# A fused state-space, attention and feed-forward kernel: the opening of attention on VectorE with the residual's seeds in eight transfers, and a last stage that takes its output products by alternating quarters

## What is computed

```python
def block_one(x):                       # stage A: a selective scan (Mamba)
    xz = x @ in_proj_w.T ; conv ; silu ; softplus steps ; scan over 512 positions, 16 states
    return y * silu(z) @ out_proj_w.T

def _gate(x, Wsel):                     # sigmoid scores, the best 2 of 8 experts kept
    s = jax.nn.sigmoid(jnp.einsum('bsd,hed->bhse', x, Wsel))
    _, idx = jax.lax.top_k(s, K)
    return s * jax.nn.one_hot(idx, E).sum(-2)

def _moe_attn(x, Wq, Wk, Wv, Wo, Wsel_v, Wsel_o):     # stage B
    q, k = _rope(x @ Wq), _rope(x @ Wk)               # 16 heads of 64
    v = jnp.einsum('bsd,bhse,hedp->bhsp', x, _gate(x, Wsel_v), Wv)
    att = softmax(q k^T / sqrt(64))
    return jnp.einsum('bhsp,bhse,hepd->bsd', att @ v, _gate(x, Wsel_o), Wo)

src = _ln(src + _moe_attn(src, ...), ln1_g, ln1_b)    # stage C
src = _ln(src + relu(src @ W1 + b1) @ W2 + b2, ln2_g, ln2_b)

x = x + _layernorm(block_one(_layernorm(x)))
x = x + _layernorm(block_two(_layernorm(x)))
```

## Time and profile before

| | |
|---|---|
| median of 3 runs | 3919.82 us (3918.64 to 3920.61) |
| the profiled execution's own time | 3914.3 us |
| its span | 3912.5 us |
| PE busy | 3596.8 us (92%) |
| PEld busy | 2472.4 us (63%) |
| DVE busy | 3211.4 us (82%) |
| ACT busy | 2037.4 us (52%) |
| POOL busy | 2722.2 us (70%) |
| mean granted TensorE clock | 0.980 |

### The profile page before, as it was taken

The page is one execution under the profiler, slowest core; times in us unless marked ns, Lnnn a source line. Parts: engine busy times, 40 slices in busy tenths (PEclk is TensorE's granted clock), DMA queues, the critical chain, the costliest instruction groups (busy, mean ns, idle before and its releaser), DMA issues. The chain is left out here.

```text
span 3912.5 us, 55524 instructions
## 1 busy us (share of the span) xinstructions
PE 3596.8 (92%) x15792; PEld 2472.4 (63%) x15792; DVE 3211.4 (82%) x3580; ACT 2037.4 (52%) x3795; POOL 2722.2 (70%) x2852
## 2 busy tenths in 40 slices
PE   6999999998669999999999999999999999999797
PEld 3444444444247777777777777777777777777586
DVE  6999989998748888888888887888887888888697
ACT  5666666666334454445454545444444445444455
POOL 4877788787657676677777677767677767776344
PEclk9999999999979999999999999999999999999898
DMA  2110111011043242323232323233323332222111
GB/s 78 54 49 27 65 70 71 20 56 60 25 159 81 56 110 55 81 60 105 55 87 78 77 64 100 60 76 89 76 60 77 88 73 68 66 70 68 43 33 49
DMA packets 76054, 267.78 MB, mean 68 GB/s; under 512 B 9326, under 2 KB 38894, under 8 KB 53072
## 3 DMA queue, kind: packets, MB, share of 16 engines
q1 hardware_dynamic: 74944, 262.83, 24.8%
q0 software_dynamic: 1040, 4.19, 0.3%
HBM read 247.85 MB, written 19.14 MB: 68 GB/s over the span
## 5 line engine op out<-in xcount | busy, mean ns | idle before, releaser
L384 POOL TENSOR_TENSOR state<-state,c_rows 128x1024 f32<-128x1024 f32 x256 | 604.6, 2365 | 215.1 <-DVE state L848 212.7
L848 DVE TENSOR_TENSOR_SCAN state<-dA,ps_a 128x1024 f32<-128x1024 f32 x256 | 585.2, 2286 | 46.8 <-PE ps_a L524 21.8
L1104 POOL TENSOR_TENSOR qk_full<-vg 128x512 f32<-128x512 f32 x256 | 330.1, 1289 | 254.3 <-DVE vg L1489 254.1
L715 ACT ACTIVATE dA<-dt,a_neg 128x511 f32<-128x511 f32 x512 | 338.8, 714 | 311.4 <-DVE state L848 309.5
L1489 DVE TENSOR_TENSOR vg<-ps_b,gates 128x1024 f32<-128x1024 f32 x256 | 313.6, 1225 | 221.2 <-PE ps_b L1215 188.6
L524 PE MATMUL ps_a<-state,ident 128*128 128x512 f32 x1024 | 481.9, 593 | 0.4 <-POOL state L384 0.4
L1213 PE MATMUL ps_b<-ogT_high,wo_high 128*128 128x512 f32 x1024 | 415.6, 406 | 33.8 <-POOL ogT_low L1117 27.2
L1378 ACT ACTIVATE prob<-ps_b,negmax 128x512 f32<-128x512 f32 x512 | 343.6, 676 | 188.9 <-DVE negmax L1495 188.9
L1213 PE MATMUL ps_b<-wv_high,xT_high 128*128 128x512 f32 x1024 | 414.3, 405 | 3.8 <-POOL wv_low L1097 3.8
L1215 PE MATMUL ps_b<-ogT_high,wo_low 128*128 128x512 f32 x1024 | 408.2, 399 | 0.0
L1214 PE MATMUL ps_b<-ogT_low,wo_high 128*128 128x512 f32 x1024 | 405.9, 396 | 0.0
(11 more groups left out here) (245 smaller groups left out, 8449.9 us busy)
## 6 DMA issues: line engine op xcount, KB each, us to landing
ogT_low<-gates_scratch SPq DMA_DIRECT2D x128, 512.0 KB, 6.3
wide_high<-gates_scratch SPq DMA_DIRECT2D x128, 512.0 KB, 9.7
xT<-xT_scratch SPq DMA_DIRECT2D x65, 512.0 KB, 3.3
c_rows<-c_scratch SPq DMA_DIRECT2D x32, 1024.0 KB, 5.4
wv<-in_wv SPq DMA_DIRECT2D x8, 1024.0 KB, 11.5
wo<-in_wo SPq DMA_DIRECT2D x8, 1024.0 KB, 13.5
x_in<-in_x SPq DMA_DIRECT2D x8, 512.0 KB, 5.1
x_a<-in_x SPq DMA_DIRECT2D x8, 512.0 KB, 7.1
```

Of the source, the lines that this page charges most:

```text
L384: pool.tensor_tensor(state, state, c_rows[:, n, :].unsqueeze(1).to_broadcast([P, HALF, S]), ALU.mult).then_inc(hc_done, 1)
L715: act.activation(dA[s % RING][:, m, 1:S], dt[par][:, HALF * f + m, 1:S], ACT.Exp, scale=a_neg[:, HALF * f + m, n:n + 1]).then_inc(dA_done, 1)
L848: dve.tensor_tensor_scan(h[s % RING][:, :, :].rearrange("p c s -> p (c s)"), dA[s % RING][:, :, :].rearrange("p c s -> p (c s)"), ps[:, DB ...
L1104: pool.tensor_tensor(v4[:, at, :, :], vg[:, at, 0:4, :], vg[:, at, 4:8, :], ALU.add).then_inc(vsum_done, 1)
```

## The change

It has two parts that don't touch each other.

Stage B, ahead of batch 0: the low parts of `xT`, `wqk` and `wv` are made by VectorE (`low_start`) instead of GpSimd, and two of the four maxima stand ahead of those of `wv`, so that GpSimd has only the rank chain. For this, `first` and the scores of batch 0 alone are loaded early (`rank_loaded`) and the other seven batches' scores later. The 4 MB seed on GpSimd's queue becomes eight of 512 KB on SyncE's (`load_seed(b)`, behind `widen` of batch b of the first pair), and the addition to `acc` waits for its own batch's. ScalarE's table load goes ahead of its first copy. SyncE's code for the first pair is written out on its own.

Stage C: TensorE takes output blocks 0 to 5 of quarter 0, then 0 to 5 of quarter 2, then 6 and 7 of each, then quarter 1, then the transposes, then quarter 3. `finish` on GpSimd also waits until VectorE has written `a` (line 1943).

```diff
@@ block.sync, stage B
-            def pair(j, more):
+            def pair(j, more, seeds=False):
                 sp.wait_ge(xT_low, CREDIT + j * NB + 1)
                 load_xT(1)
                 widen(j * NB)
+                if seeds:
+                    load_seed(0)
...
+            def load_seed(b):
+                sp.wait_ge(acc_loaded, CREDIT + b * 16)
+                sp.sem_inc(held, 1)
+                sp.dma_start(acc[:, bass.ds(b, 1), :, :], d["xT"][bass.ds(b, 1)].rearrange("b p k s -> p b k s")).then_inc(acc_loaded, 16)
...
             load_weights(0, ("wqk",))
+            sp.dma_start(first[:, :], d["first"]).then_inc(rank_loaded, 16)
+            sp.dma_start(scores_in[:, 0:TT, :], d["scores"][0, :, 0, :, :]).then_inc(rank_loaded, 16)
             for n, t in (("sin", sin), ("cos", cos)):
                 sp.dma_start(t[:, :, :], d[n]).then_inc(tables_loaded, 16)
             load_weights(0, ("wv",))
-            sp.dma_start(first[:, :], d["first"]).then_inc(scores_loaded, 16)
-            load_scores(0)
+            sp.dma_start(scores_in[:, TT:NB * TT, :], d["scores"][0, :, 1:NB, :, :].rearrange("p b t c -> p (b t) c")).then_inc(scores_loaded, 16)
             load_weights(0, ("wo",))
-            with sp.Fori(0, PAIRS - 1) as j:
-                pair(j, True)
+            pair(0, True, True)
+            with sp.Fori(0, PAIRS - 2) as r:
+                pair(r + 1, True)
@@ block.gpsimd, stage B
             def start():
-                low_wqk(0)
-                low_half(0, "wv", 0)
-                low_half(0, "wv", 1)
                 rank_one(0, 0)
                 rank_two(0, 0)
                 rank_three(0)
                 rank_four(0, 0)
-
-                pool.dma_start(acc[:, :, :, :], d["xT"].rearrange("b p k s -> p b k s")).then_inc(acc_loaded, 16)
...
-            low_x(0)
             turns(pool, start, batch, pair_start)
@@ block.scalar, stage B
             def start():
-                act.preload_act_table_set("natural_log_exp_and_others")
...
+            act.preload_act_table_set("natural_log_exp_and_others")
             high_x(0)
@@ block.vector, stage B
+            def low_start(high, count, low, done):
+                dve.wait_ge(high[0], count)
+                dve.tensor_tensor(low[1], low[0], low[2].bitcast(F32), ALU.subtract).then_inc(done, 1)
+
             def start():
+                low_start((xT_high,), 1, (xT_in[:, :, :], xT[1][:, :, :], xT[0][:, :, :]), xT_low)
+                low_start((w_high["wqk"],), 1, (w_in["wqk"][:], wqk[1][:], wqk[0][:]), w_low["wqk"])
+                dve.wait_ge(rank_loaded, 32)
+                top_of(0, 0, grouped(scores_in[:, 0:TT, :]))
+                top_of(0, 1, rank[:, :, :])
+                low_start((w_high["wv"],), 1, (w_in["wv"][:, 0], wv[1][:, 0], wv[0][:, 0]), w_low["wv"])
+                low_start((w_high["wv"],), 2, (w_in["wv"][:, 1], wv[1][:, 1], wv[0][:, 1]), w_low["wv"])
+                top_of(0, 2, left[:, :, :])
                 dve.wait_ge(tables_loaded, 32)
                 turn_raw(0)
+                top_of(0, 3, rank[:, :, :])
                 swap_halves(0)
                 rotate(0)
                 low_qk(0)
-                for k in range(TOPS):
-                    tops(0, 0, 0, k)
...
-                dve.wait_ge(acc_loaded, 16)
+                dve.wait_ge(acc_loaded, CREDIT + b * 16 + 16)
@@ stage C
-            def finish(c):
+            def finish(c, rows_ready=None):
+                if rows_ready is not None:
+                    pool.wait_ge(a_done, rows_ready)
...
-                    finish(i - 2)
+                    finish(i - 2, i + 2 if lo == 0 else None)
...
-            def outputs(i, t):
-                for m in range(FB):
+            def outputs(i, t, blocks=range(FB)):
+                for m in blocks:
...
-                outputs(i, 0)
+                for blocks in (range(BY_POOL), range(BY_POOL, FB)):
+                    outputs(i, 0, blocks)
+                    outputs(i, 2, blocks)
                 outputs(i, 1)
...
-                outputs(i, 2)
                 outputs(i, 3)
```

More of the change, by code:

```diff
@@ L975, in stage_b @@
         tables_loaded, scores_loaded, acc_loaded = sem("tables_loaded"), sem("scores_loaded"), sem("acc_loaded")
+        rank_loaded = sem("rank_loaded")
         top_done, rank_step, gates_done, held = sem("top_done"), sem("rank_step"), sem("gates_done"), sem("held")
@@ L1009, in _ @@
         def _(sp):
-            for s in (v_psum, s_psum, out_psum, acc_done, vsum_done, scaled, wide_loaded, gT_stored, xT_low, top_done, rank_step):
+            for s in (v_psum, s_psum, acc_loaded, out_psum, acc_done, vsum_done, scaled, wide_loaded, gT_stored, xT_low, top_done, rank_step):
                 sp.sem_inc(s, CREDIT)
@@ L1047, in pair @@
                     widen(j * NB + r + 1)
+                    if seeds:
+                        load_seed(r + 1)
                 sp.wait_ge(xT_low, CREDIT + j * NB + NB)
@@ L1053, in pair @@
                 widen(j * NB + (NB - 1))
+                if seeds:
+                    load_seed(NB - 1)
+            def load_seed(b):
+                sp.wait_ge(acc_loaded, CREDIT + b * 16)
+                sp.sem_inc(held, 1)
+                sp.dma_start(acc[:, bass.ds(b, 1), :, :], d["xT"][bass.ds(b, 1)].rearrange("b p k s -> p b k s")).then_inc(acc_loaded, 16)
             def load_scores(j):
@@ L1556, in tops @@
                 if k == 0:
-                    dve.wait_ge(scores_loaded, j * 16 + 32)
+                    dve.wait_ge(scores_loaded, j * 16 + 16)
                 top_of(it, k, (grouped(scores_in[:, bass.ds(b * TT, TT), :]), rank[:, :, :], left[:, :, :], rank[:, :, :])[k])
+            def low_start(high, count, low, done):
+                dve.wait_ge(high[0], count)
+                dve.tensor_tensor(low[1], low[0], low[2].bitcast(F32), ALU.subtract).then_inc(done, 1)
             def start():
+                low_start((xT_high,), 1, (xT_in[:, :, :], xT[1][:, :, :], xT[0][:, :, :]), xT_low)
[6 more added lines that the diff above has]
+                top_of(0, 2, left[:, :, :])
                 dve.wait_ge(tables_loaded, 32)
                 turn_raw(0)
+                top_of(0, 3, rank[:, :, :])
                 swap_halves(0)
```

## The result

The changed kernel takes 3885.95 us (3883.95 to 3886.8, 4 runs), against 3919.23 (3917.91 to 3920.61, 4 runs) for the kernel before: 33.3 us less, a ratio of 0.9918 with a 95% interval of 0.9906 to 0.993. Forecast were 26.2 us and 3893.6; the lower end of the range, 3887, is missed by 1.05 us. The profiled execution took 3886.78 us, its span 3885.0.

What follows compares the result with a forecast made beforehand. TensorE was busiest; its waits in the opening (`gates`) and stage C (`hT_low`, `a`) were priced at 9.4 + 16.8 = 26.2 us off 3914.3, giving 3888.1; plus 5.5 for the median, 3893.6, range 3887 to 3906.

Steps and rivals of the forecast that it cites:

- the two issues ahead of `wv`: Stage B opening: two more SyncE issues, 0.43 us each, delay `wv` by between 0 and 0.9 us, taken as 0.6.
- The bound passed from `gates` to `qk_low`: Stage B opening: gates come by 1116 to 1118, so TensorE next waits for `qk_low`, ending at 1118.4, 2.5 later than before.
- the middle of a fast and a slow one: Opening, turning of gates to `vg`: between 3.44 and 5.91 us by clock, putting `vg` at 1124.7, between 1123.5 and 1126.0.
- the forecast 2.5: Late in batch 0: VectorE's 2.54 us wait for the spread gates goes once the seed is off GpSimd.
- Rival (c): Opening gives almost nothing because `wv_low` and the turning queue on one engine; total about 17 to 19, 3902; chance 0.05.
- 2.7 for each of the turns 2 to 6: Stage C: these five turns each shorten by 2.7 us, 13.6 in all, from removed TensorE waits; bounds 1.6 and 3.3 each.
- the balance of both engines: Stage C steady turn: TensorE and VectorE settle between 24.6 and 26.3 us, taken as 25.2, down from 27.92.
- fewer collisions: Stage C: with VectorE later, fewer of its small steps meet GpSimd's `hT_low`; one less at 1.5 us behind, each saving about 1.
- Rival (a): Stage C: VectorE becomes the bound, collisions stay, turns of 26.3; total gain 14 to 20, 3902; chance 0.2.
- Rival (b): Stage C gives nothing: the wait moves to `aT_low`, period back to 27.9; only 9.4 left, 3910.4; chance 0.07.
- Turns 0 and 1: Stage C: the first two turns give their own smaller waits and the second halves, 3.2 us.
- Rival (d): Stage B loops: each addition to `acc` comes later by d, paid 56 times; at 0.7 us slower, 3933; chance 0.04.

Runs made afterwards that it cites:

- e5: The changed kernel with the 4 MB seed back as one transfer on GpSimd behind the first rank chain: 3882.74 us, opening 64.0 us.
- e11: Unchanged copy of e5 (changed kernel with one seed transfer on GpSimd), for one more profile: 3883.12 us in one run, opening 62.6 us.
- e3: The kernel before with only TensorE's new order of output products in stage C, without finish's wait for `a`: 3899.95 us, ratio 0.9959.
- e4: The kernel before with only `finish`'s wait for `a` added in stage C: 3908.72 us, ratio 0.9989.
- e8: The changed kernel with an extra VectorE copy ahead of every addition to `acc`: 3909.85 us, ratio 0.9982 to the kernel before.
- e0: The changed kernel once more, unchanged, on the same chip as its parts: 3885.41 us, ratio 0.9921 to the kernel before.

## Why the prediction was right, and where it was off

The mechanisms were the ones named; the gain was under-sized, 33.3 against 26.2, just past the lower end of the range. In two places the forecast was helped by luck: the clock in the opening, and turn 6 of stage C.

**Opening, 10.0 against 9.4: right, nearly step by step.** With the 6.2 us taken off, `wv_high` starts at 1106.2, so that the two issues ahead of `wv` delayed it by 0.0 and not 0.6; `qk_low` ends at 1117.7 (1118.4 forecast), the gates are turned at 1120.6 without a wait (1120 or after the scores), `vg` starts at 1124.1 (1124.7). The bound passed from `gates` to `qk_low` as said.

The clock was right only in sum. The prediction gave the scores 1.7 us, at 2.4 GHz, and the stretch from the gates to `vg` 4.6, the middle of a fast and a slow one. The scores took 2.9 at 1.2 GHz, and the stretch behind them 3.55, close to the 3.44 that it had at the higher clock: 6.4 together against 6.3. Where such a stretch is slow changes from one execution to the next, and e5 and e11, one kernel, put 1.4 us on that.

From `vg` to the first addition it is 36.6 before and 34.2 after, 2.4 of the forecast 2.5. But its reason was half of it: the wait goes because the seed is off GpSimd's queue, and e5 and e11 show that it would have gone with the seed left there, since GpSimd now comes to it earlier. Rival (c) is out.

**Stage C, 21.1 against 16.8: the term "2.7 for each of the turns 2 to 6" was too small.** Cut where TensorE starts each turn, these five took 27.90, 27.92, 27.92, 28.22 and 26.90 us and take 24.53, 24.75, 24.75, 24.75 and 23.59. That is 16.5 us in place of 13.6. (Cut at f, as in the windows above, turn 6 gives 4.28, of which 0.97 is VectorE, 1.8 us behind TensorE in the steady turns, catching up.) Two things were wrong in the term.

First, VectorE. The prediction put the balance of both engines at 25.2, between 24.6 and 26.3, and it lies at 24.75. VectorE's work shrank from 25.58 to 24.05 us, and with the 0.7 of gaps that the prediction counted this is the turn. Of its steps on 12 elements, six took over 1 us in the earlier trace rows's turn, 7.5 us together; now five do, 6.0. The rows of the turn after show how the two engines came apart: VectorE runs later against the hidden blocks, so ScalarE waits 1.43 us for `var_c`, GpSimd's `hT_low` has a hole of 1.93 us, and four of VectorE's small steps fall into it, at 0.16 each. This is what the prediction called fewer collisions; it credited them with 1.1 us (26.3 to 25.2), and 1.5 came. `f`, for which VectorE had waited 15.6 us in all, now waits 1.7, once, ahead of the last one. No run makes VectorE's turn lighter and nothing else, so that it sets the length rests on these rows and on e3, where both grew by 0.27. Rival (a) was half right: VectorE does set the length of the steady turns, but at 24.75 and not 26.3, since the collisions did not all stay. Rival (b) is out.

Second, the clock. The forecast priced a wait at its length, and took the steady turn as a measure for all five. Of the three turns of the kernel before that have matmuls at 1.2 GHz (2, 5 and 6; the first, third and fourth of its windows above), turn 2 lost nothing by it, since they filled the wait for `a`, and turn 5 lost 0.3. Turn 6 has a wait of only 1.63 us for `hT_low` and none for `a`, so that by its waits it had 1.8 us to give. It gave 3.3, because the slow matmuls had made it 1.5 longer: in e4, where its clock is 1.00, it takes 25.40 us and not 26.90. The 2.7 that the sum had for this turn came near that by luck.

Turns 0 and 1 gave 3.5 (3.2 forecast) and turn 7 gave 0.1 (0 forecast). Another 0.9 lies ahead of the first turn, in a stretch that takes 23.5 to 25.9 us in the 14 profiles with either order; no run shows it to be of the change.

**The lock.** `a` went from 3.31 to 1.23 us and `o` from 1.23 to 3.28. y runs from 3784.13 to 3787.17, `o` is issued inside it and ends at 3788.26, 1.1 behind y's end. e3 and e4 show what the place of this block is worth: 0.27 us a turn with the new order, 1.23 with the old one where the clock is the same. The rule weighed in the prediction, of the Trainium skill, SBUF — State Buffer, section "Who interferes with whom", is that the second of VectorE and GpSimd to issue is blocked for the whole of the first; by that rule `o` would start its work only at y's end, and the trace agrees, with 3.28 us for `o`.

**Rival (d)** is out: the addition starts 1.14 us behind `vg` as before and TensorE waits 29.7 us for it in 56 batches, and e8 shows that the rival's price per microsecond was right.

**The frame.** 5.5 us were added since the median of the runs shown was above the profiled execution of the kernel before. For the kernel after, that difference is -0.8. By the traces the two parts give 10.0 + 21.1, which is 31.0 before rounding; the medians on one chip give 31.0 too (e0), those of the first comparison 33.3, with an interval from 27 to 37. So some 5 of the 7 us by which the forecast fell short are the two parts, and the rest is not told apart from the spread of the executions.

## What to carry to other kernels

A gap of TensorE costs its length and sometimes more: look at the granted clock of the window behind it before pricing its removal. When two engines block each other by turns, their busy times are no constants; a new phase between them changes them, here by 1.5 of 25.6 us, so that a bound made of busy time is soft on both sides. A busy share near 100% does not name the limit: here TensorE is listed at 24.68 of 24.74 us, and the length is VectorE's. And two edits that remove one wait are worth that wait once: try each alone before keeping both, and cut the traces at marks that the edits don't touch, since the end of an untouched stage lay up to 8 us apart here from one profile to another.

## What the runs showed that I had not expected

The same instructions, after gaps of the same length, came back to 2.4 GHz at different times: the opening in 62.6 to 63.0 us or in 64.0 to 64.6, and the turns of e4 in 26.70 or 27.93. What decides it in an execution stays open; no experiment here controls it. The Trainium skill, TensorE: Matmul & The Clock Gate, Part 1 on the clock gate, says that the same kernel runs a different number of its first matmuls at the lower clock from one run to the next. The trace agrees, with e5 and e11, one kernel, at 64.0 and 62.6 us, and it shows the same behind gaps in the middle of the work.
